# The two residual sums of a fused token, attention and expert layer: on VectorE in place of POOL

## What is computed

```python
h = tok(ids, mask, dist)                      # h = silu(norm([embed, neighbours] @ w1 + b1)) @ w2 + b2
x = layernorm(h)
comb = phase_memory(x) + key_value_memory(x)  # the attention part, causal over the 512 tokens
h = h + x + (layernorm(comb) * ln_g + ln_b) @ out_w + out_b
h = h + experts(layernorm(h))                 # 2 of 8 experts for each token, hidden width 128
```

## Time and profile before

| | |
|---|---|
| median of 3 runs | 175.92 us (175.77 to 176.03) |
| the profiled execution | 175.03 us |
| its span, first to last instruction | 173.3 us |
| mean granted TensorE clock | 0.910 |
| TensorE, VectorE, ScalarE, POOL busy | 145.1, 121.9, 76.5, 15.1 us |
| the chain that ended last, by engine | PE 60%, DVE 29%, ACT 5%, issue 4% |

### The profile page before, as it was taken

The page is one execution under the profiler, slowest core; times in us unless marked ns, Lnnn a source line. Parts: engine busy times, 40 slices in busy tenths (PEclk is TensorE's granted clock), DMA queues, the critical chain, the costliest instruction groups (busy, mean ns, idle before and its releaser), DMA issues.

```text
span 173.3 us, 2294 instructions
## 1 busy us (share of the span) xinstructions
PE 145.1 (84%) x781; PEld 85.8 (49%) x781; DVE 121.9 (70%) x348; ACT 76.5 (44%) x126; POOL 15.1 (9%) x41
## 2 busy tenths in 40 slices
PE   5799999999923974999768968469999999699981
PEld 2273744547922224668657435146558535344520
DVE  6999999794898989998898999973226494050101
ACT  2010351666582509647913222427252734825540
POOL 5404000740001600000000000000000000000000
PEclk9956999999975567559999999999999999999999
DMA  4999923000000000000000000000000000002011
GB/s 122 349 424 430 419 114 109 12 0 0 0 0 4 0 0 0 0 4 0 0 4 0 0 0 4 2 0 0 0 4 0 0 0 0 0 19 45 0 30 30
DMA packets 3778, 9.21 MB, mean 53 GB/s; under 512 B 2356, under 2 KB 2484, under 8 KB 3256
## 3 DMA queue, kind: packets, MB, share of 16 engines
q1 hardware_dynamic: 3768, 9.08, 14.0%
HBM read 8.55 MB, written 0.52 MB: 52 GB/s over the span
## 4 chain that ended last, share of the span: by engine, by line
PE 60%; DVE 29%; ACT 5%; issue 4%; POOL 0%; DVEq 0%; ACTq 0%; POOLq 0%
PE bank L930 9%; PE bank L914 6%; PE bank L628 5%; PE bank L915 4%; PE bank L606 3%; PE bank L691 3%; DVE invpos L991 2%; PE bank L779 2%; PE bank L706 2%; PE bank L619 2%; PE bank L703 2%; PE bank L699 2%; PE bank L708 1%; DVE q_sc L1223 1%; DVE proj L1110 1%
## 5 line engine op out<-in xcount | busy, mean ns | idle before, releaser
L559 ACT ACTIVATE hid<-bank 128x512 f32<-128x512 f32 x32 | 17.9, 599 | 21.4 <-PE bank L915 21.3
L572 PE MATMUL bank<-spin 128*128 128x512 bf16 x67 | 17.9, 406 | 6.1 <-POOL spin L324 2.0
L1350 DVE TENSOR_TENSOR h<-bank,h 128x256 f32<-128x256 f32 x4 | 1.7, 423 | 21.7 <-PE bank L941 21.7
L930 PE MATMUL bank<-hid,ffn_sb 128*64 128x512 f32 x64 | 16.8, 614 | 0.0
L914 PE MATMUL bank<-xp,w1hi 128*128 128x512 f32 x32 | 14.7, 458 | 0.4 <-ACT xp L543 0.4
L572 PEld LDWEIGHTS bank<-spin 128*128 128x128 bf16 x67 | 6.5, 106 | 14.3 <-DVE hc L1312 2.3
L915 PE MATMUL bank<-xp,w1lo 128*128 128x512 f32 x32 | 12.7, 395 | 0.0
L1248 DVE TENSOR_TENSOR dist_sb<-bank,fold_sb 128x256 f32<-128x256 f32 x16 | 6.0, 419 | 7.8 <-PE bank L784 6.9
L914 PEld LDWEIGHTS bank<-xp,w1hi 128*128 128x128 f32 x32 | 6.0, 188 | 8.6 <-ACT hid L559 4.4
L1032 DVE TENSOR_TENSOR dist_sb<-dist_sb,mask_in 128x1024 f32<-128x1024 f32 x8 | 9.2, 1211 | 0.0
L628 PE MATMUL bank<-dist_sb,neigh 128*64 128x512 f32 x32 | 9.1, 678 | 0.0
(11 more groups left out here) (266 smaller groups left out, 333.9 us busy)
## 6 DMA issues: line engine op xcount, KB each, us to landing
dist_sb<-in_dist SPq DMA_DIRECT2D x4, 1024.0 KB, 11.3
mask_in<-in_mask SPq DMA_DIRECT2D x2, 512.0 KB, 8.1
fold_sb<-in_folded SPq DMA_DIRECT2D x1, 998.0 KB, 11.0
ffn_sb<-in_ffn SPq DMA_DIRECT2D x1, 816.0 KB, 17.8
late_sb<-in_late SPq DMA_DIRECT2D x1, 728.5 KB, 16.3
mask_in<-in_mrows SPq DMA_DIRECT2D x1, 512.0 KB, 3.2
out<-h SPq DMA_DIRECT2D x8, 64.0 KB, 1.7
early_sb<-in_early SPq DMA_DIRECT2D x1, 167.0 KB, 2.3
```

The source lines that it names most:

```text
L559: nc.scalar.activation(hid[:, at % HB], bank[hid_bank[at % 3]][:, :], ACT.Gelu).then_inc(S["hid_set"], 1)
L572: nc.tensor.matmul(bank[i][:, :], spin[:, 0:P], spin[:, :], start=True, stop=True)
L930: mm = nc.tensor.matmul(bank[2][j * D:(j + 1) * D, :], K["e_w2"][:, (e + j) * D:(e + j + 1) * D], hid[:, (at + j) % HB], start=False, stop ...
```

## The change

The two instructions leave POOL's list. VectorE gets a function `residual(g)` that does the same two sums on the same tiles, with the same waits and a wait for `h_set` besides. For pair 0 it is called in `project(0)`, between the copies of the gate values (lines 1122 and 1124) and the third and fourth copy out of `joint` (line 1116). For pair 1 it is called in `chunks(1)`, behind the last masked scores and the last chunk state (lines 1248 and 1259) and ahead of the variance (line 1272). POOL's `project` keeps only its `yield`s, and `pool_step` is gone.

```diff
             def project(g):
                 yield
-                pool.wait_ge(S["fused_set"], 1)
-                pool.wait_ge(S["x_set"], g + 1)
-                pool.wait_ge(S["xt_mm"], g + 1)
-                nc.gpsimd.tensor_tensor(v8(x[:, g]), v8(h[:, g]), v8(x[:, g]), ALU.add).then_inc(pool_step, 1)
-                pool.wait_ge(pool_step, g + 1)
-                nc.gpsimd.tensor_tensor(v8(x[:, g]), v8(x[:, g]), rows_bc(row_bias[:, :], 8),
-                                        ALU.add).then_inc(S["hx_set"], 1)
                 yield
...
+            def residual(g):
+                dve.wait_ge(S["fused_set"], 1)
+                dve.wait_ge(S["xt_mm"], g + 1)
+                dve.wait_ge(S["h_set"], g + 1)
+                dve.wait_ge(S["x_set"], g + 1)
+                link(nc.vector.tensor_tensor(v8(x[:, g]), v8(h[:, g]), v8(x[:, g]), ALU.add))
+                nc.vector.tensor_tensor(v8(x[:, g]), v8(x[:, g]), rows_bc(row_bias[:, :], 8),
+                                        ALU.add).then_inc(S["hx_set"], 1)
...
                 nc.vector.tensor_scalar(zg[:, g, 32:40], bank[1][:, 32:40], K["sg_b2"], None, ALU.add).then_inc(S["zg_set"], 1)
+                if g == 0:
+                    residual(0)
                 joint(2, 3)
...
                     masked(c)
                     chunk_state(c - 1)
                     yield
+                if g:
+                    residual(1)
                 yield
                 dve.wait_ge(S["var_mm"], g + 1)
```

More of the change, by code:

```diff
@@ L250, in tower @@
         stored = sem("stored")
-        dve_step, pool_step = sem("dve_step"), sem("pool_step")
+        dve_step = sem("dve_step")
         names = """spin_set pos_set ones_set w1_centred w2_centred out_centred tables_mm tables_set ids_set spread_mm onehot_set neigh_mm neigh_set diag_off
```

## The result

| | before | changed |
|---|---|---|
| median | 175.95 us (175.77 to 176.03, 4 runs) | 173.83 us (173.06 to 174.07, 4 runs) |
| the profiled execution | 175.03 us | 173.06 us |
| its span | 173.3 us | 171.3 us |
| mean granted TensorE clock in it | 0.910 | 0.890 |

The ratio is 0.9873, with a 95% interval of 0.984 to 0.9907. The medians lie 2.12 us apart, and the two profiled executions 1.97.

What follows compares the result with a forecast made beforehand. VectorE's contiguous work was taken to set the pace around pair 1's stall. From the median, 175.92 - 1.93 (stall) - 0.2 (clock) = 173.8 us, other terms costing nothing; range 173.1 to 175.0.

Steps and rivals of the forecast that it cites:

- The stall of pair 1: VectorE's running sum and product, lines 1110 and 1111, drop from 3.83 to 1.90 us, 1.93 less on the chain.
- remainders of POOL's instructions: At pair 1, VectorE's holds measured against the ends of POOL's sums: 1.17 and 1.02, together 2.19 us.
- Passed on to line 1188 and to TensorE: VectorE reaches line 1188 at 63.03, not 64.96; TensorE starts line 699 at 65.54, not 67.47, with 1.48 us idle left.
- The stall of pair 0 costs nothing: At 34 to 37 us, 1.95 us of VectorE's time is freed but covered by TensorE's work: no gain.
- The four added instructions: VectorE's new sums take 0.69 us each, about 1.42 per pair, hidden in waits before 43.11 and line 1272.
- The clock, gaining side: From 65.54 us, TensorE's first 1.4 us of work meets full clock; adds 0 to 0.84 us, 0.2 taken.
- prediction's own sign of being wrong: Granted clock from 67 to 82 us unlike a 2 us shift, or line 1116's pair starting later than 43.2.
- The clock, losing side: Full clock returns only at 77.16 and none is had before 66.9 us; 0.97 us is lost.
- Nothing happens: Stretched instructions at 56 us have another cause, or ScalarE's GELU wasn't behind the arctangent: 175.9 us, chance 0.05.
- Cover lost at pair 0: Line 1116 and TensorE delayed by the full 1.42 us: 175.4 us, chance 0.05.
- Slower by the clock: Full clock returns later than before, at 81 us where the stage ends: net 1.0 slower, 176.9 us, chance 0.07.
- The clock takes part back: Full clock returns no earlier than before, nothing had at 65.54: gain 0.96, 174.96 us, chance 0.18.

Runs made afterwards that it cites:

- pair 1 alone: Changed kernel with pair 0's two sums back on POOL, only pair 1's on VectorE: 173.73 us beside 175.64, ratio 0.9894.
- later POOL: Kernel before with all four sums still on POOL, started later, when VectorE has no instruction with two SBUF inputs: 173.74 us beside 175.64, ratio 0.9889.
- POOL writes: Changed kernel with five POOL memsets of an unused tile at the old moment of pair 1's sums: 173.64 us beside 175.50, ratio 0.9889.
- POOL's additions put back: Changed kernel with POOL doing pair 1's two additions again at the old moment, into an unused tile: 175.48 us beside 175.50, ratio 1.0008.
- sums left out: Changed kernel with the sums done by nobody and all waits for `hx_set` gone: 173.24 us beside 175.64, ratio 0.9877.
- more at pair 0: Changed kernel with two more VectorE additions of the same size behind pair 0's sums: 173.79 us beside 175.50, ratio 0.9896.
- more at pair 1: Changed kernel with three more VectorE additions, 2.13 us, behind pair 1's sums: 173.39 us beside 175.58, ratio 0.9883.
- six fillers less: Changed kernel without six unread TensorE products ahead of pair 0's transposes of h3: 172.55 us beside 175.58, ratio 0.9857.
- five fillers more: Changed kernel with five more unread TensorE products ahead of the last outputs of pair 0's chunks: 172.71 us beside 175.58, ratio 0.9837.
- pair 0 alone: Changed kernel with pair 1's two sums back on POOL, only pair 0's on VectorE: 175.77 us beside 175.64, ratio 1.0006.
- kernel before with five fillers: Kernel before, POOL's sums unchanged, with five more unread TensorE products ahead of the last outputs of pair 0's chunks: 175.36 us beside 175.63, ratio 0.9996.
- pair 1's sums at the old place: Changed kernel with pair 1's two sums on VectorE directly behind pair 1's product, about where POOL did them: 175.07 us beside 175.50, ratio 0.9971.

## Why the prediction was right

The predicted median was 173.8 us, and 173.83 was measured. The mechanism that carries the number, 1.93 us of VectorE's stall, came as forecast. That the two agree to 0.03 us is luck. The interval of the ratio allows a gain of 1.6 to 2.8 us, and five further versions without pair 1's hold (pair 1 alone, later POOL, POOL writes, more work at either place) gained 1.8 to 2.1 by their ratios. Step by step:

- *The stall of pair 1.* Predicted 3.83 to 1.90 us; measured 1.22 + 0.69 = 1.91, so 1.92 went and not the 2.19 of the remainders of POOL's instructions. The runs with POOL's additions moved in time, put back for nobody, and replaced by writes show the cause by itself.
- *Passed on to line 1188 and to TensorE.* Predicted 63.03 and 65.54; measured 63.00 and 65.51, with 1.63 us of idle time left where 1.48 were predicted (the products before it end at 63.88 instead of 64.06, as the clock rises a little earlier).
- *The stall of pair 0 costs nothing.* Right: the run with pair 1 moved alone keeps it and has the full gain.
- *The four added instructions.* Predicted 0.69 us each and covered; they take 0.68 and 0.69. Twice as many at pair 0 overrun by 0.13 us, and two and a half times as many at pair 1 still fit.
- *The clock, gaining side.* The prediction had the first 1.4 us of TensorE's work meet full rate, bounded the further gain by VectorE's two waits of 0.42, and took 0.2. Line 692 met full rate for about 1.0 us, the wait before line 1147 shrank from 0.42 to 0.17, and the schedule stood 2.42 us ahead at 80.89 in place of 1.96: 0.46 more. The other 0.2 of it came ahead of line 1144 (1140 of before), in what the prediction took for VectorE's contiguous work. The prediction's own sign of being wrong, a granted clock from 67 to 82 us that is no mere shift by 2 us, did show: a shift asks for half rate from about 65.0 to 75.2 us, 10.2 in all, and it stood from 66.6 to 73.4, for 6.8. The clock part of the prediction was wrong in this; it lacked a reason for how long half rate would last.
- *The clock, losing side.* Here the prediction looked at the wrong stretch. It feared a loss between 67 and 77 us, where there was a gain. In the profiled execution the loss came at 90.5 to 100.7: fourteen filling products ran at 0.43 us each, line 854 ended at 101.4, and VectorE waited 0.52 us. The 2.42 us became 1.94, the 118.39 - 116.45 at which the first masked scores of pair 1 now start. So between the profiled executions the clock gave 1.97 - 1.93 = 0.04 us and not the 0.2 of the prediction. It doesn't do so in all executions:

  | profiled execution of | half rate between 90 and 104 us | start of pair 1's running sum to `hc` | wait ahead of `hc` |
  |---|---|---|---|
  | changed kernel; pair 1 alone; sums left out | 10.2 us | 45.43; 45.41; 45.42 us | 0.51 to 0.52 us |
  | POOL later; POOL writes; more at pair 0; more at pair 1; six fillers less | 6.8 us | 44.90 to 44.93 us | none |
  | five fillers more | none | 44.91 us | none |
  | kernel before; POOL's additions put back | none | 47.34; 47.35 us | none |
  | pair 0 alone; kernel before with five fillers | 6.8 us | 46.87; 47.29 us | none |

  The run with pair 1's sums at the old place had 10.2 us of half rate too, and a wait of 0.53 us. The 45.4 us are the 47.34 of before less the 1.93 of the stall. So the clock gave the changed schedule either nothing or 0.5 us in all, and half rate for 6.8 us cost nothing where 10.2 us cost 0.5. The 0.2 of the prediction lies between the two by chance; it was not foreseen in its parts.
- *The rivals.* Nothing happens: ruled out by pair 1 alone. Cover lost at pair 0: ruled out by the 0.80 us left there. Slower by the clock: not seen. The clock takes part back: in some executions, by 0.5 us and elsewhere, which there cancelled what it had given before.

What stays open is what makes the clock fall near 90 us and how long half rate then lasts. In the changed kernel's trace TensorE is idle for 1.31 and 0.69 us before the fall, as in the kernel before at 89.7 and 91.9, where the clock did not fall. But it fell at 93.7 us with pair 0 moved alone and at 94.2 us in the kernel before with five fillers, so the place was not a safe one in the old schedule either. No run varied the shift alone.

## What to carry to other kernels

An instruction on a helper engine is not free because nobody waits for its result: look at what the other engine runs in the same microseconds, and compare its instructions with the same shapes elsewhere in the trace. Where a hold shows, it can be taken away by moving the work to another engine's idle time or by moving it in time on the same engine; both gave 1.9 us here. Read TensorE's clock from more than one trace: in almost the same schedule half rate behind 90 us lasted 10.2 us, 6.8 us or not at all, and only the longest cost time. One profile before and one after would have put this down to the change.

## What the hardware showed that was not expected

An 8-element VectorE instruction of 0.17 us is held as long as a 512-column one, for 1.0 us, if it meets POOL's addition.

Executions of one kernel differ by about 1 us with the mean granted clock, and at first sight not in the direction one would think: over all sets the kernel before took 175.4 to 176.2 us in the executions with a mean of 0.93, and 174.6 to 175.3 in those with 0.88 or 0.89; the changed kernel took 174.03 and 174.07 at 0.928, and 173.06 at 0.890. Middle against middle (175.8 and 174.95) the change gives 1.8 and 1.9 us.

The mean misleads here. The run with POOL's writes was profiled at 0.927, and its view shows 1.00 for all of the first 51 us. But TensorE's timeline of it has

```profile
1.98 3.17 PE L581 MATMUL bank<-spin 128*128 128x512 bf16 x7 [1.98 <-POOL spin L325]
5.62 1.09 PE L594 MATMUL bank<-thn 4*100 4x512 bf16 x2 [0.47 <-DVE thn L1004]
```

Seven filling products in 3.17 us are 0.45 us each. That is the pace at half rate (0.43 in the 14 products at 95.02 us), and twice the 0.23 at full rate (14 products in 3.18 us in the kernel before, at 95.26). The changed kernel's trace has the same 3.17 us, also beside a shown 1.00. So the 1.00 that a view shows ahead of the first fall it records need not be full rate. Behind that the two differ: the pair of products at 5.6 us takes 1.09 us in the run with POOL's writes and 0.63 in the changed kernel, and the sixteen neighbour products (14.18 and 13.46 us) take 5.04 and 4.55. The execution with the higher mean was the one whose TensorE ran longer at half rate at its start. It is 1.21 us late at the first folded product (19.15 against 17.94), 1.08 at pair 1's running sum (57.17 against 56.09), 0.55 at `hc` (102.07 against 101.52, where the changed kernel waits), and 0.53 at the end. That the other executions with a mean near 0.93 are of this kind is inferred from their means alone.
